# First attention: minus the maxima sent to all partitions by DMA instead of by TensorE and ScalarE, the queries' projection copied by ScalarE and split by VectorE, the sums one step later

## The reference, cut to what matters

```python
x = x + attn_ref(layernorm(x), W_qkv, b_qkv, W_out, b_out)     # 16 heads x 64, positions added to the keys
x = x + ffn_ref(layernorm(x), ...)                              # second attention, router, 4 experts
# in attn_ref
qkv = x @ W_qkv + b_qkv
k = k + pos_enc[None, :, None, :]
scores = jnp.einsum('bqhd,bkhd->bhqk', q, k) / scale
attn = jax.nn.softmax(scores, axis=-1)
out = jnp.einsum('bhqk,bkhd->bqhd', attn, v).reshape(b, s, H * D)
return out @ W_out + b_out
```

## Time and profile before

| | |
|---|---|
| median of 3 runs | 2247.55 us (2245.63 to 2248.91) |
| the profiled execution's own time | 2247.04 us |
| its span, first to last instruction | 2245.2 us |
| granted TensorE clock, mean over the span | 0.974 of full speed |
| busy, share of the span | PE 93%, DVE 78%, ACT 78%, POOL 55% |
| one chunk of the first attention (from one `m_rows` to the next, 31 of them from 70.3 to 1349.8 us) | 41.3 us |

### The profile page before, as it was taken

One profiled execution on the slowest core, in us unless ns is written; L12 is line 12 of the kernel. 1 busy time (PEld: TensorE's weight loads), 2 busy tenths in 40 slices (PEclk: granted clock), 3 DMA queues, 4 the chain that ended last, 5 costly groups with the idle time before them and its releaser, 6 DMA issues.

```text
span 2245.2 us, 35828 instructions
## 1 busy us (share of the span) xinstructions
PE 2099.1 (93%) x12074; PEld 934.2 (42%) x12074; DVE 1741.8 (78%) x2794; ACT 1757.7 (78%) x2387; POOL 1226.4 (55%) x763
## 2 busy tenths in 40 slices
PE   5899999999999999999999999899999999999997
PEld 2444444444444444444444443333333333333334
DVE  5677777787787777777777775789999999999913
ACT  1588888888888888888888888268878888888882
POOL 1477777777777687687687688332113025006003
PEclk8799999999999999999999999679999999999998
DMA  3000000000000000000000000000000000000000
GB/s 119 1 1 1 1 1 1 1 1 1 1 1 1 1 1 1 1 1 1 1 1 1 1 20 1 1 1 1 2 1 1 2 1 6 2 2 6 1 1 10
DMA packets 12270, 11.30 MB, mean 5 GB/s; under 512 B 2112, under 2 KB 10944, under 8 KB 11968
## 3 DMA queue, kind: packets, MB, share of 16 engines
q1 hardware_dynamic: 12096, 9.01, 1.3%
HBM read 7.69 MB, written 1.05 MB: 4 GB/s over the span
## 4 chain that ended last, share of the span: by engine, by line
PE 61%; DVE 16%; ACT 13%; issue 6%; POOL 1%; DVEq 0%; ACTq 0%; POOLq 0%
PE acc_o L523 11%; PE acc_o L644 10%; PE scores L630 9%; PE scores L493 8%; ACT prob L830 6%; DVE mxp L1343 5%; PE ring L468 5%; DVE accp L1377 5%; ACT scores L838 3%; DVE mxp L1449 3%; ACT prob L861 2%; PE ring L689 2%; PE ring L610 2%; PE ring L697 2%; PE ring L542 2%
## 5 line engine op out<-in xcount | busy, mean ns | idle before, releaser
L1008 POOL TENSOR_TENSOR accp<-accp,prob 128x1024 f32<-128x1024 f32 x318 | 809.1, 2544 | 61.7 <-ACT prob L830 22.4
L1343 DVE TENSOR_REDUCE mxp<-ring 128x1 f32<-128x512 f32 x1024 | 648.1, 683 | 176.0 <-PE ring L468 166.3
L861 ACT ACTIVATE prob<-scores 128x512 f32<-128x512 f32 x1024 | 544.1, 599 | 136.0 <-PE scores L630 133.7
L830 ACT ACTIVATE prob<-scores 128x1024 f32<-128x1024 f32 x512 | 520.0, 1016 | 132.0 <-PE scores L493 109.5
L493 PE MATMUL scores<-q_all,k_all 64*128 64x512 f32 x3072 | 556.8, 408 | 6.4 <-ACT scores L838 4.9
L1449 DVE TENSOR_REDUCE mxp<-ring 128x1 f32<-128x512 f32 x789 | 510.1, 683 | 50.2 <-PE ring L610 34.2
L838 ACT ACTIVATE scores<-minus_all 128x1024 f32<-128x1024 f32 x510 | 524.5, 1029 | 26.3
L523 PE MATMUL acc_o<-prob,v 128*64 128x512 f32 x2048 | 497.4, 606 | 0.0
L468 PE MATMUL ring<-k_all,q_all 64*128 64x512 f32 x1024 | 412.3, 438 | 56.2 <-DVE q_all L1329 24.4
L493 PEld LDWEIGHTS scores<-q_all,k_all 64*128 64x128 f32 x3072 | 340.3, 186 | 64.1 <-ACT scores L838 26.1
L630 PE MATMUL scores<-q_all,k_all 32*128 32x512 f32 x1024 | 304.7, 494 | 13.0 <-ACT prob L861 8.8
(11 more groups left out here) (189 smaller groups left out, 1657.4 us busy)
## 6 DMA issues: line engine op xcount, KB each, us to landing
w_all<-w_pairs SPq DMA_DIRECT2D x1, 1344.0 KB, 11.1
pos_sb<-pos SPq DMA_DIRECT2D x1, 1024.0 KB, 5.8
w_sb<-w SPq DMA_DIRECT2D x4, 256.0 KB, 4.6
mrow<-m_rows SPq DMA_DIRECT2D x64, 2.0 KB
w_all<-w SPq DMA_DIRECT2D x1, 1024.0 KB, 5.4
q_all<-m_rows SPq DMA_DIRECT2D x64, 2.0 KB
out<-ff SPq DMA_DIRECT2D x4, 256.0 KB, 2.2
wout_sb<-wout_pairs SPq DMA_DIRECT2D x1, 512.0 KB, 7.6
```

The costliest lines, as they stand in the source:

```text
L830: nc.scalar.activation(prob[:, T % SLOTS1, :, :], sc[T % 2][:, :, :], ACT.Exp, scale=SCALE1).then_inc(exp_done, 1)
L861: nc.scalar.activation(prob2[:, h // 2, T % 2, h % 2, :], sc2[place % 3], ACT.Exp, scale=SCALE2).then_inc(exp2_done, 1)
L1008: nc.gpsimd.tensor_tensor(accp[:, k % 2], accp[:, k % 2], prob[:, T % SLOTS1], ALU.add).then_inc(pool_acc, 1)
L1343: done(nc.vector.reduce_max(mxp1[k % 2][:, h * QT + q, kc:kc + 1], bank[:], AX.X), ("max", k, q, kc, h))
```

## The change

Five edits. (1) SP no longer fills `mrow` for each chunk, but sends each of the 8 rows of `m_rows` to all 128 partitions of `minus_all` itself (8 DMAs of 128 x 128 for a chunk, two buffers of `minus_all` in turn); the two matmuls of `minus` and ScalarE's two copies go. `mrow` and its two DMAs stay for chunk 0 alone, whose first two tiles aren't seeded. ScalarE's seeds of a new chunk wait for all 8 DMAs. (2) ScalarE copies the queries' projection with its bias to SBUF (`qf`) and so frees the bank; VectorE makes `qhi` from `qf` (a copy with rounding) and `qlo` (a subtraction). (3) `Q` moves from step 2 to step 1. (4) `sums` moves from step 1 to step 2. (5) The reciprocals move from one in each of steps 2 to 5 to one in steps 3 and 4 and two in step 5.

```diff
 def last_item1(k, j):
-    if j == 1 and k > 0:
+    if j == 1 and k + 2 < CHUNKS1:
+        return ("Q", k + 2)
+    if j == (2 if k < LAST1 else 1) and k > 0:
         return ("sums", k - 1)
-    if j == 2 and k + 2 < CHUNKS1:
-        return ("Q", k + 2)
...
-    if j == 5 and k + 1 < CHUNKS1:
-        return ("minus", k + 1)
...
 def recip_quarters(k, j):
     if k < LAST1:
-        return [j - 2] if 2 <= j < 2 + QT else []
+        return {3: [0], 4: [1], 5: [2, 3]}.get(j, [])
...
+        def minus_spread(k):
+            return 16 * (2 + 2 * QT * (k + 1))
...
# TensorE
-                if t < 2:
-                    pe.wait_ge(m_dma, 32 * (k + 1))
+                if t == 0:
+                    pe.wait_ge(m_dma, minus_spread(0))
...
-            def minus(k):
-                pe.wait_ge(m_dma, 32 * (k + 1))
-                for h in range(2):
-                    bank = begin(("minus", k, h))
-                    end(nc.tensor.matmul(bank[:], onesw[half(h), :], mrow[half(h), k % 2, :], start=True, stop=True),
-                        ("minus", k, h))
...
# ScalarE
-                nc.scalar.activation(qhi[:, c, :], ring[bank_of(("Q", k))][:], ACT.Identity,
-                                     bias=bqk_all[:, p, 0:1]).then_inc(qh_ready, 1)
+                if k > 0:
+                    act.wait_ge(ql_ready, k)
+                wait_full(act, ("Q", k))
+                nc.scalar.activation(qf[:], ring[bank_of(("Q", k))][:], ACT.Identity,
+                                     bias=bqk_all[:, k // NC, 0:1]).then_inc(free[bank_of(("Q", k))], 1)
...
             def seed(T):
                 if T % NT < 4:
-                    for h in range(2):
-                        wait_free(act, ("minus", T // NT, h))
+                    act.wait_ge(m_dma, minus_spread(T // NT))
                 act.wait_ge(exp_done, T - 1)
-                nc.scalar.activation(sc[T % 2][:, :, :], minus_all[:], ACT.Copy).then_inc(seeded, 1)
+                nc.scalar.activation(sc[T % 2][:, :, :], minus_all[:, T // NT % 2], ACT.Copy).then_inc(seeded, 1)
-            def minus_copy(k):
...
# SyncE
             for k in range(CHUNKS1):
                 wait_free(sp, ("fin", k))
+                if k == 0:
+                    for h in range(2):
+                        sp.dma_start(mrow[64 * h:64 * h + 1, :].bitcast(F32),
+                                     m_rows[QT * h:QT * (h + 1), :].bitcast(F32)).then_inc(m_dma, 16)
+                elif k >= 2:
+                    sp.wait_ge(seeded, NT * (k - 1) - 2)
                 for h in range(2):
-                    sp.dma_start(mrow[64 * h:64 * h + 1, k % 2, :].bitcast(F32),
-                                 m_rows[QT * h:QT * (h + 1), :].bitcast(F32)).then_inc(m_dma, 16)
+                    for q in range(QT):
+                        row = m_rows[QT * h + q:QT * h + q + 1, :].bitcast(F32)
+                        sp.dma_start(minus_all[:, k % 2, h, q * 128:(q + 1) * 128],
+                                     row.unsqueeze(1).to_broadcast([1, 128, 128])).then_inc(m_dma, 16)
...
# VectorE
-                bank = open_(("Q", k))
+                wait_free(dve, ("Q", k))
+                nc.vector.tensor_copy(qhi[:, c, :], qf[:]).then_inc(qh_ready, 1)
                 dve.wait_ge(qh_ready, k + 1)
-                done(nc.vector.scalar_tensor_tensor(qlo[:, c, :], bank[:], bqk_all[:, p, 0:1], qhi[:, c, :].bitcast(F32),
-                                                    ALU.add, ALU.subtract), ("Q", k))
+                nc.vector.tensor_tensor(qlo[:, c, :], qf[:], qhi[:, c, :].bitcast(F32), ALU.subtract).then_inc(ql_ready, 1)
```

More of the change, by code:

```diff
@@ L138, in start1 @@
             + [("K", 0, 2)] + tiles[1] + [("K", 0, 3), ("V", 0, 2), ("V", 0, 3)] + tiles[2] + [("Q", 1)] + tiles[3]
-            + [("rows",)] + early[:3] + [("fin", 0)] + early[3:] + [("minus", 0)])
+            + [("rows",)] + early[:3] + [("fin", 0)] + early[3:])
 def uses1():
@@ L147, in use @@
             uses.extend([("max", *it[1:], h) for h in range(2)])
-        elif it[0] == "minus":
-            uses.extend([(*it, h) for h in range(2)])
         else:
@@ L280, in build @@
         qhi, qlo = q_all[:, 0:NC, :], q_all[:, NC:2 * NC, :]
-        mrow = sb("mrow", [128, 2, CW], F32R)
-        minus_all = sb("minus_all", [128, 2, CW])
+        mrow = sb("mrow", [128, CW], F32R)
+        minus_all = sb("minus_all", [128, 2, 2, CW])
+        qf = sb("qf", [128, CW])
         onesw = sb("onesw", [128, 128], F32R)
@@ L563, in item1 @@
                     sums(it[1])
-                elif kind == "minus":
-                    minus(it[1])
                 else:
@@ L744, in _ @@
                     pe.wait_ge(pairs_dma, 16 * 3)
[L745 to L748, removed]
                 item1(it)
+            pe.wait_ge(blank, 4)
+            scores(0)
+            scores(1)
             for k in range(CHUNKS1):
@@ L807, in v_copy, with queries @@
                                      .rearrange("p (t n) -> p t n", t=QT), ACT.Copy).then_inc(free[bank_of(("V", p, b))], 1)
[L809 to L810 removed]
+            def queries(k):
+                if k > 0:
+                    act.wait_ge(ql_ready, k)
                 wait_full(act, ("Q", k))
[L812 to L813 removed]
+                nc.scalar.activation(qf[:], ring[bank_of(("Q", k))][:], ACT.Identity,
+                                     bias=bqk_all[:, k // NC, 0:1]).then_inc(free[bank_of(("Q", k))], 1)
             def sums_copy(k):
@@ L929, in _ @@
                 elif it[0] == "Q":
-                    rounded_queries(it[1])
+                    queries(it[1])
             exps(0)
             exps(1)
-            minus_copy(0)
             seed(2)
@@ L953, in _ @@
                         sums_copy(it[1])
-                    elif it and it[0] == "minus":
-                        minus_copy(it[1])
                     elif it and it[0] == "Q":
-                        rounded_queries(it[1])
+                        queries(it[1])
                     for it in LATE1.get((k, j), []):
```

14 lines of the change are left out of this document (7 added, 7 removed).

## The result

The changed kernel takes 2820.43 us (median of 4 runs, 2816.59 to 2836.24) against 2248.23 us (2245.63 to 2249.12) for the kernel before, run beside it: 1.2563 times as long, 95% interval 1.2542 to 1.2584. So it is 572 us slower. The forecast was 2764, in a range of 2200 to 2870.

A forecast was written before the change was run, and what follows sets the result against it. TensorE was busy 93% of the span, so only waits were left to gain. 14.0 - 0.5 + 0.9 + 1.7 = 16.1 us for 31 chunk changes (499), plus 17 at the start, gave 2764 us, range 2200 to 2870.

The forecast's parts named there:

- The serial reads, +14.0: At each chunk change, 8 DMAs read one partition at 20 ns a packet; seeds wait, step 7's values come 14.0 us later.
- the store's 288 GB/s: A store from all 128 partitions with same-size packets reached 288 GB/s; evidence for quick, hidden `minus_all` DMAs.
- Rival (a): `minus_all` DMAs: repeated reads go twice as fast, 10 ns a packet; +4.2 us a chunk, 2385 us; chance 0.08.
- (b): `minus_all` transfers hidden; step 5 to 6 shrinks by 1.3 us; 2238 us, or 2200 without the subtraction's wait; chance 0.20.
- (c): Transfers hidden, but VectorE's pair on the queries waits for GpSimd in full; +0.9 us a chunk, 2275 us; chance 0.08.
- (d): Transfers hidden, and gains and waits cancel over the chunk; 2248 us; chance 0.04.
- The clock, +1.7: After TensorE idles for the DMAs in each chunk, it runs 3.4 us at half clock, costing 1.7 us.
- `Q` and the sums, +0.4: Steps 1 to 3: `sums` no longer waits for VectorE's add, -0.5 us; queries' split through `qf` costs +0.9 a chunk.
- I take half of the mean: VectorE's subtraction on `qf` waits 0 to 2.4 us for GpSimd; half the mean, giving +0.9 us for `Q` in all.
- no one-input operation of VectorE in this trace does so: Argument against VectorE's copy within SBUF also waiting for GpSimd, up to another 2.4 us.
- The start, +17: At the kernel's start, score tiles wait for all ten DMAs, until 94.1 instead of 76.73: +17 us.
- the case's own range: Range of the serial-reads case: 13.5 us a chunk gives 2683 us, 20.7 gives 2906; chance of the case 0.60.

The follow-up runs named there:

- e3: The changed kernel, but each of a chunk's 8 DMAs copies 128 rows of zeros from 128 partitions instead of one row 128 times: 2346.59 us.
- e5: The changed kernel, but each of the 8 DMAs reads four neighbouring partitions of zeros, 32 times each: 2920.72 us.
- e6: The changed kernel, but each of the 8 DMAs reads four partitions of zeros that are four apart, 32 times each: 2374.69 us.
- e7: The kernel before with only the steps of `Q`, `sums` and the reciprocals moved; queries split and `minus` as before: 2223.32 us.
- e2: The kernel before with the edits on `Q` (copy through `qf` and move), `sums` and the reciprocals, `minus` left on TensorE and ScalarE: 2372.3 us.
- e8: The kernel before with only the queries' copy to `qf` and VectorE's two instructions on it, no steps moved: 2378.35 us.
- e9: e7 with VectorE making both parts of the queries straight from the PSUM bank, without ScalarE's part: 2225.01 us.
- e4: The changed kernel, but each of the 8 DMAs reads one 512 B row of HBM (the output bias) 128 times: 2661.11 us.
- e1: The changed kernel with `Q`, `sums` and the reciprocals as before, so the `minus_all` DMAs alone: 2701.31 us.

## Why the prediction was right, and where it was off

**The serial reads, +14.0: right, and shown.** 18.0 ns a packet instead of 20, so the last DMA lands 20.1 us behind `m_rows` (mean of 30 chunks) instead of 22.1. The mechanism, one group of neighbouring partitions gives 26 GB/s whoever asks, stands by e3 (many partitions: 4.7 ns) and by e5 against e6. Of the doubts, that four packets are few, and the store's 288 GB/s, the first came to nothing, and the second was read at all partitions at once and did not apply. Rival (a), twice the rate, would have landed at 11.9 us; (b), (c) and (d) need the transfers hidden, which only the kernels that read from far-apart partitions came near.

**The clock, +1.7: right, as near as the steps tell.** From the first seed's start to step 7's values it took 5.75 us in the chunk shown (1048.75 to 1054.50) and 5.4 on average, where the prediction summed 4.3, and step 7 to 0 takes 5.93 instead of 5.07. Together that is 2.0 us. 0.3 of it is something else, which the prediction held to be hidden ("Step 6, its item"): in 14 of the 31 chunks, as in the one shown, the item of step 6 is a `V` projection; ScalarE's copy `v` then stands between the second seed and the next exponentials, TensorE waits 0.6 us for its bank, and the values come after 5.75 us instead of 5.15 at most. The other 1.7 fits the matmuls at half clock; no run separates it. With the landing 2.0 earlier, the sum for steps 5 to 0 is 14.0 - 2.0 + 2.0 = 14.0, forecast 15.7, measured 14.1. `minus` itself gave back 1.2 us in step 5 to 6 (5.48 to 4.26), close to rival (b)'s 1.3, and all of it lies inside the wait.

**`Q` and the sums, +0.4 together: the mis-sized term.** Steps 1 to 3 grew by 4.0 us a chunk. The moves alone gave 1.0 (e7) instead of 0.5. The split through `qf` cost 4.8 in their place (e2 less e7, 149 us over 31), and 4.2 without them (e8), where the prediction had 0.9. It failed in three steps.

First, "I take half of the mean": the subtraction does not meet GpSimd at random. Its median is 2719 ns of a largest 2722, so it waits 2.03 us in 29 of 32 chunks. It follows VectorE's copy at once, GpSimd's next add has just begun when that copy ends (e2's timeline), and it stands behind nearly all of this add. The trace of the kernel before had such a regular wait in the earlier trace rows: VectorE's add of step 0 takes some 2.72 us in nearly every chunk (median 2721 ns of 31) and that of step 1 some 1.21 (median 1207), so which operation waits is set by the order of the work and not by chance. Rival (c) had a wait in full at `Q`, +2.7, and even that is short of 4.8.

Second, "no one-input operation of VectorE in this trace does so" was true, but it did not carry over to the copy. One such operation reads fp32 in SBUF (`ssum`) in the kernel before, in 44 of its 124 cases wholly within one of GpSimd's adds, and never waits:

```profile
L1384 DVE RECIPROCAL rec<-ssum x124: 894/942/944, 136.4 to 1391.4; 128x128 f32<-128x128 f32 x124
```

The new copy (`CAST`) does: it takes 0.43 us alone, less than the 0.69 of the copy from PSUM by which the prediction priced it, and 1.10 at the median. So one input in SBUF is not what decides, and the trace of before held no copy within SBUF to read this from.

Third, the clock was counted at the DMA's wait only; the 3.3 us wait here lowers it as well, and 4.6 us at half clock in e2 are some of the 4.8. Which share each has was not separated: e9 takes away all three at once. The steps give a hint: of the 5.0 us between e7 and e2, 3.1 stand in step 1 to 2, with the wait, and 1.9 in step 2 to 3, which lies behind it.

The Trainium skill, "SBUF — State Buffer", section "Who interferes with whom", says that copies and casts can enter a mode that takes the port pair shared with GpSimd, for the whole instruction, and that an instruction with two inputs in SBUF also contends with GpSimd's reads. The prediction weighed the first and set it aside; the runs side with the page, as `CAST` and e9 (same work, input in PSUM: 0.75 us each time) show.

**The start, +17:** 93.30 for the expected 94.1, so +16.6.

**The sum.** Forecast 16.1 a chunk, measured 18.2 by the steps of chunks 2 to 29 and 18.0 over all 31. The 56 us by which 2764 is short come from two errors against each other: steps 1 to 3 are short by 3.6 a chunk, steps 5 to 0 too long by 1.6. So part of the closeness is luck: with the landing right and the rest as it stood, the forecast would have been some 62 us lower, near 2700. The upper end of the case's own range, 20.7 a chunk, leaves out the 0.5 of `sums`: by the terms it is 20.2 and 2890 us.

**What the profile was to show.** ScalarE idle before one seed a chunk, released by the DMA: 438.0 us in 31 waits. DMA at 26 GB/s for 20 us: 28 for 18.45. TensorE's share 76%: 80, since its busy time grew at half clock, which the forecast of the share did not count. No wait for `minus_all`, or at `sums` for VectorE: none.

## What to carry to other kernels

The broadcast by DMA ran here at the rate at which its source gave its rows (28 GB/s from one partition, 86 from four that are four apart): look at the partitions that the packets leave, not at bytes or at the number of DMA engines. Sixteen copies of the row, 8 partitions apart, made the same transfer nearly four times as fast (4.8 ns a packet instead of 18.0), and a wider reduction and transpose made them. And before an operand is moved from PSUM to SBUF to free a bank, see whether GpSimd is adding there: an instruction that follows another on VectorE can stand behind nearly all of one of GpSimd's adds in nearly every chunk (2.0 us here), and the wait of 3.3 us that this made on TensorE was followed by 3.4 us at half clock.

## What the runs showed of the hardware that was not expected

- One row of HBM read 128 times gave 39 GB/s (13.0 ns a packet of 512 B, e4).
- Four neighbouring partitions gave less than one: 21.4 ns a packet (e5) against about 18 (the change, e1).
- SP's issues took longer where the transfers ahead were slow. In the changed kernel an issue takes 1882 ns at the median and the 8 of the chunk shown take 13.45 us (the first three 0.47 to 0.60 each, the next three 2.2 to 2.5), where the same instruction took 0.53 us with four partitions that are four apart (e6). SP's list of the tile in the changed kernel (ns, least, median, largest):

```profile
L1238 SPq DMA_DIRECT2D minus_all<-m_rows x256: 469/1882/3189, 72.7 to 1921.2; - x128
```

- Behind a wait of TensorE of 3.3 us its clock stood at 0.51 for 3.4 us. In the 14 us before, which hold 2.6 us of that wait, it had been busy for 11.1 at full clock (e2).
